# Degrees counted in the first half of stage one, folding inside the sums stage, table weights made in the expert stage

## The reference, cut to what matters

```python
edge_index = jnp.stack([src, dst])
xn = _layernorm(x)
x = x + _L0_gnn_ref(xn, src, dst, ...) + _L0_mix_ref(xn[None], ...)[0]
x = x + _L0_ffn_ref(_layernorm(x)[None], ...)[0]
xn = _layernorm(x)
x = x + _L1_gnn_ref(xn, edge_index, ...) + _L1_mix_ref(xn[None], ...)[0]
x = x + _L1_ffn_ref(_layernorm(x)[None], ..., L1_ffn_edge_index)[0]
```

## Time and profile before

| what | value |
|---|---|
| median of 3 runs | 4448.03 us (4445.95 to 4449.41) |
| profiled execution, its own time | 4443.94 us |
| span of that execution | 4442.2 us |
| granted clock, mean over the span | 0.916 of full speed |
| PE busy | 3555.7 us (80%) |
| DVE busy | 3146.5 us (71%) |
| POOL busy | 2791.1 us (63%) |
| ACT busy | 2405.8 us (54%) |

### The profile page before, as it was taken

One profiled execution on the slowest core, in us unless ns is written; L12 is line 12 of the kernel. 1 busy time (PEld: TensorE's weight loads), 2 busy tenths in 40 slices (PEclk: granted clock), 3 DMA queues, 4 the chain that ended last, 5 costly groups with the idle time before them and its releaser, 6 DMA issues. The chain is left out here.

```text
span 4442.2 us, 67327 instructions
## 1 busy us (share of the span) xinstructions
PE 3555.7 (80%) x17780; PEld 2268.9 (51%) x17780; DVE 3146.5 (71%) x10069; ACT 2405.8 (54%) x5553; POOL 2791.1 (63%) x2880
## 2 busy tenths in 40 slices
PE   6698999999999998788878778854377777777773
PEld 5555566666666665444444445443144444444442
DVE  7776666565656664788888888875667777777777
ACT  7343323333233332599999964434466666666664
POOL 0274677576665400477777777754777777777775
PEclk9998999999999999899999999965689899898986
DMA  3333222121221101655555556534222222222221
GB/s 102 82 89 113 44 40 46 32 46 33 44 44 29 28 1 37 185 140 143 145 143 144 144 151 162 158 89 109 34 40 40 40 40 39 40 40 40 39 39 28
DMA packets 290605, 331.30 MB, mean 75 GB/s; under 512 B 79040, under 2 KB 244929, under 8 KB 290233
## 3 DMA queue, kind: packets, MB, share of 16 engines
q0 software_dynamic: 105328, 175.77, 19.3%
q1 hardware_dynamic: 184904, 151.23, 12.3%
HBM read 289.56 MB, written 30.77 MB: 72 GB/s over the span
## 5 line engine op out<-in xcount | busy, mean ns | idle before, releaser
L3186 POOL DMA_INDIRECT st_rows<-tabr,router_rsrc x1072 | 1030.6, 961 | 329.8 <-issue 318.5
L2516 POOL DMA_INDIRECT all_XT<-tab,graph_gsrc x880 | 843.7, 959 | 272.6 <-issue 232.1
L1476 POOL DMA_INDIRECT st_rows<-tab,graph_gsrc x748 | 733.3, 980 | 384.4 <-issue 203.6
L1731 ACT ACTIVATE st_h<-st_ph,st_shift,st_scale 128x448 f32<-128x448 f32 x448 | 324.4, 724 | 744.7 <-PE st_ph L1592 744.4
L2546 PE MATMUL st_po<-all_XT,st_hot 128*128 128x264 f32 x1760 | 517.5, 441 | 105.5 <-DVE gat_sum L2756 102.4
L3243 PE MATMUL st_py<-st_w,st_hid 128*128 128x256 f32 x1568 | 441.2, 430 | 2.4 <-ACT st_hid L3291 2.4
L2756 DVE TENSOR_TENSOR gat_sum<-gat_sum,st_po 128x264 f32 x880 | 375.7, 427 | 71.2 <-PE st_po L2546 2.3
L2546 PEld LDWEIGHTS st_po<-all_XT,st_hot 128*128 128x128 f32 x1760 | 299.1, 202 | 248.3 <-issue 112.8
L3231 PE MATMUL st_px<-all_XT,st_w 128*128 128x512 f32 (+2 forms) x832 | 396.6, 624 | 15.1 <-ACT st_hid L3291 15.1
L3205 PE MATMUL st_pad<-st_adr,st_hott 128*128 x1072 | 68.1, 175 | 399.4 <-DVE st_zd L3357 386.3
L1605 PE MATMUL st_po<-all_XT,st_h 128*128 128x256 f32 x1568 | 371.9, 386 | 8.5 <-DVE all_X L1922 6.7
(11 more groups left out here) (546 smaller groups left out, 7291.8 us busy)
## 6 DMA issues: line engine op xcount, KB each, us to landing
st_bc<-drowr SPq DMA_DIRECT2D x268, 128.0 KB
st_bc<-drow SPq DMA_DIRECT2D x220, 128.0 KB
st_rows<-tabr,router_rsrc POOLq DMA_INDIRECT x1072
all_XT<-tab,graph_gsrc POOLq DMA_INDIRECT x880
st_xtb<-xtd SPq DMA_DIRECT2D x98, 128.0 KB
st_rows<-tab,graph_gsrc POOLq DMA_INDIRECT x748
xtd<-all_XT SPq DMA_DIRECT2D x49, 128.0 KB, 1.7
all_XT<-xtd SPq DMA_DIRECT2D x49, 128.0 KB
```

The source lines that it names most:

```text
L1476: g.indirect_dma_start(self.rows[:, b, u, :], None, self.R.tab0, bass.IndirectOffsetOnAxis(self.R.gsrc[:, t:t + 1], 0)).then_inc(self.s_ro ...
L1731: a.activation((self.h1, self.h2)[l][:, fb, h * HALF:(h + 1) * HALF], self.ph[:, m % 3, 0:HALF], ACT.Relu, bias=self.shift[:, l, i:i + 1], ...
L2516: g.indirect_dma_start(self.rows[:, b, u, :], None, self.R.tab1, bass.IndirectOffsetOnAxis(self.R.gsrc[:, t:t + 1], 0)).then_inc(self.s_ro ...
L3186: g.indirect_dma_start(self.rows[:, b, u, :], None, self.R.tabr, bass.IndirectOffsetOnAxis(self.R.rsrc[:, t:t + 1], 0)).then_inc(self.s_ro ...
```

## The change

**Front.** The 52 batches no longer go one per step beside the tiles. Four come first (`EARLY`), then two per tile in tiles 0 to 23 (`PACE`, `DEGREES` = 24), and none in tiles 24 to 48. The steps are now counted in tiles, and the graph tables start at 23, 25, 27, 29, 31, split at 41, the transposes of slots at 42 to 48. The maximum, root and reciprocal of the degrees stand at tiles 24 and 25. Table 0's parts are made at tiles 26, 27, 29, 31, 37, 44 and behind the last (`SCALE_AT`), with a cast and a cut one step later and the third part two steps later. Tiles from 28 on are scaled by ACT in its copy (`taken` with `scale`), so `scaled` on DVE goes for three groups. In SP's queue the windows' transfer stands at tile 35, slot rows at tile 44, and each group's store three tiles after its scaling, all among the stores of transposed tiles.

**Prelude.** `kc` has four buffers, and the products run three tiles late. The product with ones goes: in place of it the last key column of each tile is set to 1, and behind the loop two products with the matrices `full` and `tail`, made at the start, recover the lost column and the sums. The multiply-add on DVE goes into ACT's root (`scale`, `bias=eps`); the root also waits for `s_k1`, and so does DVE's reciprocal. Edge groups come at tile `8(q+1)//5 + 1`: 29 of the 33 in the loop, four behind it, one after each step of the folding. `fold0` is gone as a block: its instructions are at the end of Prelude's programs. The block mask is made by POOL after the fourth edge group.

**Stage1.** The statistics of a group are taken one tile at a time in steps 0 to 6 of the next, and aggregates and copies at step 7; those of the last group in pairs as its last expert ends. The extra columns are made on DVE at c = 2 and 3 (e = 3) and c = 5 (e = 3 and 5), their loads by SP at n = 1 and 4. **table1** loses loads, columns and the wait.

```diff
@@ Prelude
-    KCB = 3
+    KCB = 4
+    LAG = 3
+    def due(self, q):
+        return 8 * (q + 1) // 5 + 1
...
-            t.matmul(self.psv[:, 0:self.PAIRS * self.VCOL], R.ones[:, :], kc[:, self.HALFKV:self.KROW], start=(n == 0),
-                     stop=(n == W - 1)).then_inc(self.s_kv, 1)
+            mm.then_inc(self.s_kv, 1)
...
+        for q in self.late(0):
+            edges(q)
+        t.wait_ge(self.s_matrix, 1)
+        t.wait_ge(self.s_most, 1)
+        t.matmul(self.pfull[:, 0:self.PAIRS * self.VCOL], self.full[:, :], self.most[:, :], start=True, stop=True)
+        t.matmul(self.psv[:, 0:self.PAIRS * self.VCOL], self.tail[:, :], self.most[:, :], start=True, stop=True)\
+            .then_inc(self.s_fixed, 1)
+        for q in self.late(1):
+            edges(q)
...
         def root(n):
-            a.wait_ge(self.s_var, n + 1)
-            a.activation(self.std[:, n % 2], self.ssum[:, n % 2], ACT.Sqrt).then_inc(self.s_std, 1)
+            a.wait_ge(self.s_red, n + 1)
+            if n >= 2:
+                a.wait_ge(self.s_k1, n - 1)
+            a.activation(self.std[:, n % 2], self.ssum[:, n % 2], ACT.Sqrt, bias=self.eps[:, 0:1], scale=1.0 / HC0)\
+                .then_inc(self.s_std, 1)
...
-            v.wait_ge(self.s_red, n + 1)
-            v.tensor_scalar(s, s, 1.0 / HC0, LN_EPS, ALU.mult, ALU.add).then_inc(self.s_var, 1)
...
+            st.then(v.memset(k4[:, :, P - 1:P], 1.0))
@@ Front
-    TILE_AT = HALVES - W
-    COUNT_AT, KEYS_AT, RANKS_AT, PLACES_AT, SLOTS_AT, SPLIT_AT = 34, 36, 38, 40, 42, 50
+    EARLY, PACE = 4, 2
+    DEGREES = (HALVES - EARLY) // PACE
+    COUNT_AT, KEYS_AT, RANKS_AT, PLACES_AT, SLOTS_AT, SPLIT_AT, PUT_AT = 23, 25, 27, 29, 31, 41, 42
+    NORM_AT = DEGREES + 1
+    DIRECT = 4
+    SCALE_AT = (26, 27, 29, 31, 37, 44, W)
+    SHORT_AT, ROW_AT = 35, 44
...
+        for h in range(W):
+            for b in self.batches(h):
+                degree(b)
+            tile(h)
...
+            a.activation(self.xw[:, n, :], self.pext[:, n % 2, 0:GCN], ACT.Copy, scale=R.nsrc[:, n:n + 1])\
+                .then_inc(self.s_ec, 1)
...
+        def casts(n):
+            for i in range(ITER):
+                if self.SCALE_AT[i] == n:
+                    cast(i, 0)
+                if self.SCALE_AT[i] + 1 == n:
+                    cast(i, 1)
@@ Stage1
-                if e == 6 and c:
-                    final_statistics(c - 1)
+                if e == 3 and 2 <= c < 4:
+                    extra_columns(0, c - 2)
+                if e in (3, 5) and c == 5:
+                    extra_columns(1, e // 2 - 1)
+                if e < TPI and c:
+                    final_statistics(c - 1, (e,))
+                elif c:
+                    kept_statistics(c - 1, range(TPI))
@@ table1
-                v.wait_ge(s_w, 48)
-                for c in range(C):
-                    for k in range(2):
-                        st.then(v.tensor_tensor(wa[:, :], wext[:, c, 0:GH * GC], att[:, k, :], ALU.mult))
-                        o = GH * GC + k * GH
-                        st.then(v.tensor_reduce(wext[:, c, o:o + GH], wa[:, :].rearrange("p (h c) -> p h c", h=GH),
-                                                AXX, ALU.add))
-                v.sem_inc(s_ready, 1)
```

More of the change, by code:

```diff
@@ L326, in windows, with late @@
         return ws
+    def due(self, q):
+        return 8 * (q + 1) // 5 + 1
     def share(self, n):
-        return range(self.GROUPS * n // W, self.GROUPS * (n + 1) // W)
+        return [q for q in range(self.GROUPS) if self.due(q) == n]
+    def late(self, part):
+        left = [q for q in range(self.GROUPS) if self.due(q) >= W]
+        return left[len(left) * part // self.LATE:len(left) * (part + 1) // self.LATE]
     def run(self):
@@ new lines, in tensor @@
+        t.wait_ge(self.s_matrix, 1)
[5 more added lines that the diff above has]
+            edges(q)
+        ahead = R.ahead
+        t.wait_ge(self.s_ahead, 16 * (len(ahead.loads(self.A)) + TPI))
+        t.wait_ge(self.s_sq, W)
@@ new lines, in tensor @@
+        t.wait_ge(self.s_kc, 2 * W)
+        t.wait_ge(self.s_masked, C)
+        for k in range(C):
+            t.matmul(self.pkv[:, k, 0:D], self.bd[:, k, :], ahead.wqt[:, k, :], start=True, stop=True)
+        for k in range(C):
+            mm = t.matmul(self.pb[:, k:k + 1], self.bd[:, k, :], ahead.bq[:, k:k + 1], start=True, stop=True)
+        mm.then_inc(self.s_mixed, 1)
+        for q in self.late(2):
+            edges(q)
+        t.wait_ge(self.s_copied, 1)
+        for m in range(C):
+            for k in range(C):
+                t.matmul(self.pw[:, m, 0:D], self.rwt[:, k, m * P:(m + 1) * P], ahead.w1[:, k, :], start=(k == 0),
+                         stop=(k == C - 1))
@@ L429, in scalar @@
+        for m in range(C):
+            for k in range(C):
+                mm = t.matmul(self.pb[:, 64 + m:65 + m], ahead.w1[:, k, m * P:(m + 1) * P], self.bk[:, k:k + 1],
+                              start=(k == 0), stop=(k == C - 1))
+        mm.then_inc(self.s_folded, 1)
+        for q in self.late(3):
+            edges(q)
     def scalar(self, a):
@@ L520, in vector @@
             one_hot(q)
+        st.then(v.tensor_copy(self.full[:, :], R.ident[:, :]))
+        st.then(v.tensor_copy(self.tail[:, :], R.ident[:, P - 1:P].to_broadcast([P, P])))
+        st.then(v.tensor_reduce(self.full[:, P - 1:P], R.ident[:, P - HC0:P - 1], AXX, ALU.add))
+        st.then(v.tensor_scalar(self.full[:, P - 1:P], self.full[:, P - 1:P], -1.0, None, ALU.mult))
+        v.sem_inc(self.s_matrix, 1)
         for n in range(W + 1):
@@ L543, in vector @@
         st.then(v.scalar_tensor_tensor(R.kvsum[:, 0:self.HALFKV], rest, self.gcol[:, 1:2], prod, ALU.mult, ALU.add))
+        ahead, bd, rwt = R.ahead, self.bd, self.rwt
+        v.wait_ge(self.s_mask, 3)
+        for k in range(C):
+            v.scalar_tensor_tensor(bd[:, k, :], R.kvsum[:, k * P:(k + 1) * P], 1.0 / N, ahead.diag[:, :], ALU.mult,
+                                   ALU.mult).then_inc(self.s_masked, 1)
+        for q in self.late(1):
+            add_edges(q)
+        v.wait_ge(self.s_mixed, 1)
+        for k in range(C):
+            st.then(v.tensor_copy(rwt[:, k, :], self.pkv[:, k, 0:D]))
+            st.then(v.tensor_tensor(rwt[:, k, k * P:(k + 1) * P], rwt[:, k, k * P:(k + 1) * P], R.ident[:, :], ALU.add))
+        st.then(v.tensor_copy(self.bk[:, :], self.pb[:, 0:C]))
+        v.sem_inc(self.s_copied, 1)
+        for q in self.late(2):
+            add_edges(q)
+        v.wait_ge(self.s_ahead, 16 * (len(ahead.loads(self.A)) + TPI))
+        v.wait_ge(self.s_folded, 1)
+        v.tensor_copy(R.weff[:, :, :], self.pw[:, :, 0:D])
+        v.tensor_tensor(R.beff[:, :], self.pb[:, 64:64 + C], ahead.b1[:, :], ALU.add)
+        for q in self.late(3):
+            add_edges(q)
 class Front:
@@ L977, in vector, with parts @@
         rates(0)
-        for h in range(2, self.HALVES):
-            i, j = divmod(h - self.TILE_AT, TPI)
+        for h in range(2, self.EARLY):
+            one_hots(h)
+        def parts(h):
+            for i in range(ITER):
+                if self.SCALE_AT[i] == h:
+                    scaled(i)
+                if self.SCALE_AT[i] + 1 == h:
+                    cut(i, 0)
+                if self.SCALE_AT[i] + 2 == h:
+                    cut(i, 1)
+        for h in range(W):
+            i, j = divmod(h, TPI)
             if j == 0 and 1 <= i + 1 < ITER:
@@ L2225, in _ @@
             def _(s):
-                s.dma_start(wext[:, :, 0:GH * GC], rows(A.gat_w)).then_inc(s_w, 16)
-                for k, row in enumerate((A.gat_src, A.gat_dst)):
-                    s.dma_start(att[:, k, :], spread(row)).then_inc(s_w, 16)
                 s.dma_start(wkv, rows(A.m1_kv)).then_inc(s_kv, 16)
```

288 lines of the change are left out of this document (151 added, 137 removed).

## The result

The changed kernel takes 4406.76 us in the median of 3 runs (4402.74 to 4408.07), against 4448.03. The ratio is 0.990 with a 95% interval of 0.9886 to 0.9914: 41.3 us faster. The sign was right and the size less than half. The profiled execution of the changed kernel has a span of 4401.0 us at a mean granted clock of 0.914, against 4442.2 and 0.916.

What follows compares the result with a forecast made beforehand. Each stage has its own limit: Vector while counting, PE in the sums and expert stages. Gains 2.0 + 11.1 - 2.7 + 7.0 = 17.4 us, so 4448.0 - 17.4 = 4430.6; range 4412 to 4446.

Steps and rivals of the forecast that it cites:

- rival B: First stage: Vector and PE overlap fully, +17 us in place of +2, total 4416; chance 0.12.
- Sums stage: Key and value sums: Vector becomes the limit at 158 us, 11 above PE; 173 against 187.1, +13.7; with folding +11.1.
- the excess over the limiting engine: Sums stage: 17 us beyond PE's 170 before, about half start-up; taken as 15 after the third tile of lag.
- Rival A: Sums stage follows PE after all, Vector's pitch being partly slack: 147 + 17 = 164, +23 for 13.7, total 4421; chance 0.14.
- First stage: Degree counts and first table: same work reordered, last tile at 192, end at 202 against 203.9, +2 us; bounds +17 to -16.
- the term that I said would stay: End of the first stage: 7.4 us for landing of stores and barrier, kept because the last part waits for the last tile.
- Rival D: First stage: Scalar's 14 casts of table 0 wait for Vector and hold tile copies and PE; about 28 us, 4459; chance 0.05.
- the 20 at which I had called myself wrong: First stage's second half: the prediction is wrong if Scalar's waits there pass 20 us.
- Expert stage: Spread statistics: 5.8 us of PE waits go, 8.8 come at step 7; -2.7 us in all, bounds -9 to +5.
- Second table stage: PE's first extension product loses its 7.41 us wait for loads and vector instructions; 7.0 gained to the end, bounds 0 and 7.4.
- rival C: Second table stage: its 7 us are given back, its stores being the real end; total 4438; chance 0.14.
- Rival E: Sums stage: the clock falls, PE's 147 us take up to 294; total near 4550; chance 0.02.

## Why the prediction was wrong

Of the 23.9 us between forecast and result 14.7 lie in sums and folding, 8.8 in the expert stage and 5.2 in the first stage; 5.3 more behind the change work against them. Of all the medians that I had named, rival B's 4416 is nearest to the result, but by its number only: it had 15 us more in the first stage, where 5.2 came.

**Sums stage, the step that failed.** Its rows of PE were right (3.15 for 3.16), and so was the step that Vector becomes the limit. Two terms of Vector's side were mis-sized. First the pitch: I took 2.31 a tile, measured are 2.00, so Vector has 147 us of work and not 158. The 0.31 are three things. The multiply-add gave 0.20 where I took 0.10. The memset costs 0.13 where I took 0.20. And the 2.21 that I started from was 0.14 too long: I had taken 0.72 of idle out of 2.93, but an idle time is counted from the end of an instruction, and where nothing is waited for the next one starts before that end. In the changed kernel the next reduce starts 0.21 after the start of the last multiply, which itself lasts about 0.3.

Second the excess over the limiting engine. I carried over 15 us: 17 over PE's 170, less two for the lag. Measured are 13 over Vector's 147, near enough, but by two errors that cancel. Over Vector's own 160 the excess before was 27 and not 17, and the lag is worth 14 to 15 us (10.7 in the kernel before) and not two. So a loop with a lag of two takes 174.8 from the first memset, nearly my 173, with a pitch too long by 11 us of work and an excess of 15 that is 27 there. Rival A came nearest in this stage (23 us for a loop that gave 27.6), but its reason, PE as the limit, is not what the runs show: putting back 49 x 0.20 = 9.8 us of Vector's work costs 9.3 to 9.8, putting back 49 x 0.44 = 21.6 of PE's costs 13.

**First stage, mis-sized.** The order worked as forecast. Counting ended at 139.8, later than the 135 that I had, and the reciprocal of the degrees at 144.5 (forecast 138). The last tile was at 187.4 (192) all the same: I had put about 15 us of PE's idle time into the second half, between full overlap and none, and PE waits there 8.4 in all; and a pair of slot transposes takes 0.4 (from 187.31 to 187.43 + 0.27, and 0.43 in the pairs before), half of my 0.86, 3 us in all for seven. From the end of the last cut to the next stage it was 6.3, not 7.4: the term that I said would stay fell, since six of the seven stores are issued before the last cut ends (the sixth at 186.0). Rival D, the casts between the tile copies, did not come: Scalar's waits for Vector's scaling and cuts before them are 9.8 us in all in the trace, below the 20 at which I had called myself wrong.

**Expert stage, the sign that failed.** I had 8.8 us for the wait behind the aggregates, 1.75 five times; measured are 4.9 more (8.2 for 3.3), about 1.0 each. That alone turns the sign: 5.8 gone, 4.9 more, 1.0 at the end, and PE's idle time falls from 45.4 to 42.6. The other 3.3 of the 6.1 us are PE's busy time at the lower clock, which no term of mine held; 1.7 of them go with the block of statistics, and the rest I can't call a property of the change.

**Second table stage.** Right: 7.4 for 7.0, all carried through to its end, 67.4 us for 67.2. Nor is it given back in what follows at once: Vector's 501st instruction behind this stage starts 307.3 us after the first extension product in both kernels. As far as this shows, rival C, the stores as the real end, falls.

**Behind it.** I had the unchanged stages at nothing; they took 5.3 us more, and why is open. From the first extension product to the end the two profiles with the second table stage of before take 2684.5 and 2684.9 us, and the eleven others 2687.2 to 2691.1, with the same program behind that stage. The groups don't overlap, but two profiles are few, and the difference builds up over more than 1000 us and not at one place. So part of it may be the change's, by a path that no run shows, and part is the scatter of single profiles, 3.9 us among the eleven. It is also the scale at which a profile's 1 us terms end.

**The clock.** Rival E did not come: granted 0.97 in the sums stage with its cold start and end, and 1.00 in the middle, with PE busy 93%. The rule of the Trainium skill (TensorE: Matmul & The Clock Gate, HAM oscillation — how this bites in real kernels), by which a kernel that waits in each round can be throttled again each round, has no hold on this loop; the kernel of that section waits in a round for longer than it multiplies, and this loop does not. Where PE has real pauses, as in the folding, the clock was 0.59. But the row that I set against that rule was no evidence: in the first stage PE ran at 1.2 GHz, as the last section shows. The outcome was right, and this reason for it was luck.

**The chances.** The parts don't add up as stated: by my own conditions faster is 0.9 x 0.49 + 0.14 + 0.12 + 0.07 = 0.77, not 0.79, and D and E alone are 0.07, above the 0.06 that I gave for slower.

## What to carry to other kernels

When two engines work through the same tiles and both are nearly full, the distance in tiles between them is a term of the sum of its own: here one more tile gave 10.7 us alone and 14 to 15 after both engines' work had been cut. Take each engine's pitch from start to start in a tile without a wait, rather than taking idle time out of one with a wait. Count what a removed dependent instruction gives back as its own time and its wait. An excess belongs to the engine that it was taken over, 5 us for PE and 13 for Vector here, and does not carry over when the limit moves to the other. A spread order of small work should be placed behind what another engine waits for: moving the aggregates behind the normalisation took PE's wait from 8.2 to 3.2 us.

## What the hardware showed that I had not expected

**TensorE ran at 1.2 GHz through nearly the whole first stage, in all thirteen profiles, though their rows say 1.00.** In each trace the first record of the clock lies between 134 and 211 us, and a stretch ahead of it is given as 1.00. The products tell the clock. The same source line and the same shape, L223 with 128 columns in float32, in the kernel before: 438 ns from 60 to 196 us (busy us in total, mean ns, idle us before), and 279 ns in the second table stage, where the clock is on record at 0.95:

```profile
L223 PE MATMUL front_pt<-all_ident,all_XT 128*128 128x128 f32 x80 | 26.7, 438 | 0.9 <-ACT all_XT L211 0.9
L223 PE MATMUL tab_pt<-all_ident,tab_xn 128*128 128x128 f32 x94 | 18.5, 279 | 0.0
```

From 211 us on in that kernel, products of 128 columns in float32 take 417 ns or more where the record says 0.50, and 273 in the median where it says 1.00. So the row of 1.00 in the earlier trace rows, with PE busy 72.83 of 89.50 us, is a row at the lower level. At the first record, 186 us in the changed kernel, such products fall from 421 to 272 ns, for 3.4 us. The kernel with the first stage undone has its first record early; in the second row, its own, the clock is given as 0.50 where the kernel before, in the first row, has 1.00, and PE's busy time is the same (L223's products last 438 ns in both):

```profile
140.00:175.00 35.00, 29.59 (x282) 28.83 (x283) 28.79 (x61) 11.30 (x34) 11.89 (x7) 1.00 0.23 73
140.00:175.00 35.00, 29.61 (x275) 28.84 (x274) 28.97 (x62) 10.99 (x33) 11.89 (x7) 0.50 0.24 73
```

So the clock does not part the first stages of 203.9 and 208.9 us; the landing of the stores does, as above. In a stage that PE fills the clock does count: in the expert stage equal work, 1009 products, took PE 188.02 us at 0.98 and 184.58 at 1.00. Two profiles' stages are therefore compared by PE's busy time for equal products first, and by its idle time second.
